# Transformer and delta-rule kernel on one core: the value product ahead of the transposes of k and q, with fill matmuls, a reciprocal root and a residual sum moved behind other work

## The reference

```
x = x + 0.5 * ffn(layernorm(x))
x = x + attn(layernorm(x))      # delta-rule memory, 64-wide keys
x = x + 0.5 * ffn(layernorm(x)) # the same weights as the first
```

```
h = shift_token(x);  q, k, v = split(h @ wqkv)        # 8 heads of 64
q = l2norm(q) * qs;  k = l2norm(k) * ksc;  q, k = rotary_xpos(q, k)
o = local_attention(q, k, v)                          # window of 128, own and previous block
x = x + o @ wo
h = layernorm(shift_token(x)) * lg + lb;  a, g = split(h @ w1 + b1)
x = x + (a * gelu(g)) @ w2 + b2
```

## Time and profile before

| | |
|---|---|
| median of 3 runs | 2738.12 us (2736.51 to 2740.71) |
| the profiled execution | 2735.22 us |
| its span on the core | 2733.4 us, granted TensorE clock 0.995 |
| PE matmuls busy | 2530.3 us (93%) |
| PE weight loads busy | 2233.3 us (82%) |
| DVE busy | 1997.0 us (73%) |
| ACT busy | 1857.7 us (68%) |
| POOL busy | 1514.3 us (55%) |

### The profile page before, as it was taken

The page is one execution under the profiler, slowest core; times in us unless marked ns, Lnnn a source line. Parts: engine busy times, 40 slices in busy tenths (PEclk is TensorE's granted clock), DMA queues, the critical chain, the costliest instruction groups (busy, mean ns, idle before and its releaser), DMA issues.

```text
span 2733.4 us, 79930 instructions
## 1 busy us (share of the span) xinstructions
PE 2530.3 (93%) x29664; PEld 2233.3 (82%) x29664; DVE 1997.0 (73%) x6533; ACT 1857.7 (68%) x5192; POOL 1514.3 (55%) x1767
## 2 busy tenths in 40 slices
PE   8899999998999999999999899999998999999999
PEld 7788888887888888888767788888887888888888
DVE  7777777776777777777656777777776777777776
ACT  6767777766676777666454777776666677766665
POOL 5565566655555565555213556665554566655555
PEclk9999999999999999999999999999999999999999
DMA  3122101003000000005100000000003100000000
GB/s 117 33 79 75 49 18 52 21 20 112 14 2 3 2 2 25 2 2 195 33 19 31 2 2 2 2 2 2 2 2 113 33 2 18 18 18 18 17 18 25
DMA packets 75954, 82.18 MB, mean 30 GB/s; under 512 B 37552, under 2 KB 61872, under 8 KB 74416
## 3 DMA queue, kind: packets, MB, share of 16 engines
q1 hardware_dynamic: 70176, 75.51, 8.5%
q10 hardware_dynamic: 5392, 1.56, 0.2%
HBM read 49.53 MB, written 26.74 MB: 28 GB/s over the span
## 4 chain that ended last, share of the span: by engine, by line
PE 43%; DVE 18%; POOL 17%; ACT 9%; issue 7%; DMA 4%; SPq 1%; DVEq 0%; POOLq 0%; ACTq 0%
POOL pr L631 7%; PE bank L1111 6%; PE bank L1113 6%; PE bank L1112 6%; POOL r L618 5%; DVE pr L1714 5%; PE bank L1222 5%; PE bank L1345 4%; PE bank L1147 4%; DMA stt<-stt 3%; ACT pr L815 3%; POOL t L621 3%; PE bank L1510 2%; PE bank L1174 2%; DVE t L1680 2%
## 5 line engine op out<-in xcount | busy, mean ns | idle before, releaser
L631 POOL TENSOR_TENSOR pr<-pr,rden 128x384 f32<-128x384 f32 (+1 forms) x512 | 433.2, 861 | 502.1 <-DVE rden L1723 501.3
L815 ACT ACTIVATE pr<-pr,nb 128x192 f32<-128x192 f32 (+1 forms) x1024 | 440.2, 431 | 119.3 <-DVE nb L1714 119.2
L1111 PE MATMUL bank<-h2T,w 128*128 128x256 f32 x1408 | 405.2, 288 | 8.1 <-DVE h2T L1750 1.2
L1112 PE MATMUL bank<-h2T,w 128*128 128x256 f32 x1408 | 394.7, 280 | 0.0
L1113 PE MATMUL bank<-h2T,w 128*128 128x256 f32 x1408 | 394.6, 280 | 0.0
L1714 DVE CUSTOM_DVE_ANT_0 pr<-bank,maskb,r 128x192 f32<-128x192 f32 (+1 forms) x1024 | 356.6, 395 | 19.7 <-issue 9.9
L663 POOL TENSOR_TENSOR uTl<-t,uTh 128x256 fp32r<-128x256 f32 x288 | 219.1, 761 | 208.5 <-ACT uTh L911 207.8
L1111 PE MATMUL bank<-wqkv,hT 128*128 128x512 f32 x768 | 309.9, 404 | 12.4 <-DMA wqkv<-wqkv_split 8.5
L1812 DVE SCALAR_TENSOR_TENSOR t<-bank,b,t 128x256 f32<-128x256 f32 (+1 forms) x384 | 183.2, 480 | 174.5 <-ACT t L896 103.3
L1112 PE MATMUL bank<-wqkv,hT 128*128 128x512 f32 x768 | 304.4, 396 | 0.0
L1113 PE MATMUL bank<-wqkv,hT 128*128 128x512 f32 x768 | 302.1, 393 | 0.0
(11 more groups left out here) (244 smaller groups left out, 7326.2 us busy)
## 6 DMA issues: line engine op xcount, KB each, us to landing
wqkv<-wqkv_split SPq DMA_DIRECT2D x18, 512.0 KB, 7.2
w<-w_split SPq DMA_DIRECT2D x3, 2816.0 KB, 9.9
Y<-in_x SPq DMA_DIRECT2D x8, 512.0 KB, 8.0
out<-Y SPq DMA_DIRECT2D x8, 512.0 KB, 3.9
stt<-stt SPq DMA_DIRECT2D x224, 3.0 KB
h<-out SPq DMA_DIRECT2D x7, 512.0 KB, 4.0
out<-h SPq DMA_DIRECT2D x7, 512.0 KB, 3.0
stt<-stt SPq DMA_DIRECT2D x192, 0.0 KB
```

What stands on the lines that cost most here:

```text
L631: e.tensor_tensor(probs(j, t), probs(j, t), rden[:, 2 * j:2 * j + 2].unsqueeze(2).to_broadcast([P, 2, w]), ALU.mult).then_inc(pn_done, 1)
L815: last = e.activation(probs(j, t)[:, g, :], probs(j, t)[:, g, :], ACT.Exp, bias=nb[:, hd:hd + 1], scale=-1.0, accum_out=den[:, hd:hd + 1])
L1111: e.matmul(out, left[0], right[0], start=first, stop=False)
L1112: e.matmul(out, left[0], right[1], start=False, stop=False)
```

## The change

The PE places the value product ahead of the transposes of k and q, takes all W2 units out of the place between the scores and the projections, and puts six of them (in the last tile nine, as before) behind the transposes. DVE does the residual sum of the W2 product one tile later, behind the fourth score instruction pair, puts A0 ahead of the attention residual, and does the second addition of the value product's halves behind the first scores. ACT copies the value product and h2T of the last tile ahead of kT and qT. POOL computes LayerNorm's power behind all four normalisings instead of behind the first.

```
 POOL
                     for j in range(4):
-                        if t == 3 and j == 1:
-                            LN(L, b, 0)
                         NP(L, b, t, j)
+                    if t == 3:
+                        LN(L, b, 0)
 ACT
                     if ahead2:
                         A0(*ahead2)
+                    if t == 3:
+                        O(L, b, t)
+                        H2T(L, b, 0)
                     if ahead:
                         A2(*ahead)
                     if L == 0 and b < B - 1 and 0 < t < 3:
                         for k in (2 * t - 2, 2 * t - 1):
                             entry_apply(b + 1, k)
-                    if t == 3:
-                        O(L, b, t)
-                        H2T(L, b, 0)
 PE
-                    cuts = ((5, 9, UNITS, UNITS), (0, 4, UNITS, UNITS), (0, 4, UNITS, UNITS), (0, 4, 8, UNITS))[t]
+                    cuts = ((5, 5, 11, UNITS), (0, 0, 11, UNITS), (0, 0, 11, UNITS), (0, 0, 8, UNITS))[t]
...
                     fill(1)
                     if ahead2:
                         A0(*ahead2)
-                    if ahead:
-                        A2(*ahead, 0)
-                        A2(*ahead, 1)
                     if t:
                         PV(L, b, t)
                     else:
                         PV_first(L, b, t)
+                    if ahead:
+                        A2(*ahead, 0)
+                        A2(*ahead, 1)
                     fill(2)
 DVE
                     if t > 1:
-                        O_add(L, b, t - 1)
+                        O_add(L, b, t - 1, 0)
                     S(L, b, t, 0)
+                    if t > 1:
+                        O_add(L, b, t - 1, 1)
                     if t:
                         O(L, b, t - 1)
                     S(L, b, t, 1)
...
                     S(L, b, t, 3)
+                    if prev and t:
+                        W2(*prev, t - 1)
                     for j in range(1, 4):
...
+                    if ahead2:
+                        A0(*ahead2)
                     if t:
                         WO(L, b, t - 1)
                         halves(L, b, t - 1)
-                    if prev and t < 3:
-                        W2(*prev, t)
-                    if ahead2:
-                        A0(*ahead2)
...
                     if t == 3:
                         LN_apply(L, b, 0)
-                        O_add(L, b, t)
+                        for i in pair:
+                            O_add(L, b, t, i)
                         O(L, b, t)
                         if prev:
                             W2(*prev, t)
```

More of the change, by code:

```diff
@@ L1723, in R, with O_add @@
                 e.reciprocal(rden[:, 2 * j:2 * j + 2], den[:, 2 * j:2 * j + 2]).then_inc(rden_done, 1)
[L1725 to L1730, removed]
+            def O_add(L, b, t, i):
+                cols = slice(2 * P * i, 2 * P * i + 2 * P)
+                e.wait_ge(o_first, at(o_first, sums(L, b, t) + i + 1))
+                e.tensor_tensor(o_sum[:, cols], bank[O_BANK[1]][:, cols], o_sum[:, cols], ALU.add).then_inc(o_added, 1)
             def O(L, b, t):
@@ L1958, in sequence @@
                         halves(L, b, t - 1)
[L1959 to L1962, removed]
                     if L == 0 and b == 0 and t < 3:
```

## The result

The changed kernel takes 2852.1 us (2850.51 to 2855.8) against 2738.01 us (2736.51 to 2740.71) for the kernel before: a ratio of 1.0417, 95% interval 1.0399 to 1.0436, slower by 114 us. The direction was forecast, the size was not: the forecast was 2812 us, and the range ended at 2850.

A forecast was written before the change was run, and what follows sets the result against it. A ring of dependences, not PE, bounds the kernel: 28 sequences at +2.0 us (56), odd sequences 4 and 1, first pass 13, together 74 on 2735.2, plus 2.9 to the median: 2812 us; range 2765 to 2850.

The forecast's parts named there:

- The ring: In the attention tiles PE, POOL, DVE and ACT wait for each other in a circle; any lengthened piece is paid in full.
- N: The end of POOL's last normalising in a tile; before the change the next S came 7.0 us later.
- Rival 1: The value product starts right behind PTE (N + 2.65) without waiting for DVE: faster, 2706 us; chance 0.10.
- S: The start of the first scores on DVE in a tile; from it to the third 1/sum took 4.7 us before.
- S at N + 7.7: DVE's first scores follow its first addition by 0.34 us, at N + 7.7 instead of N + 7.0: +0.7 us.
- The split of the two additions: Only the first addition stands ahead of S; the second (0.34 us) moves behind S in tiles 2 and 3.
- The feed-forward residual, +0.34 us in each tile: On DVE the residual moves from idle time into the stretch from S to N in tiles 1, 2 and 3.
- Tile 3, +0.4: N moves by 0.1 us against S, and the first W1 product comes at N + 9.9 instead of N + 9.6.
- rival 3: POOL's normalising locks out DVE's rotation addition in tiles 1 to 3, 0.6 us each: 2862 us; chance 0.05.
- The first pass, 13 us: ACT's normalisation of x delays its copy of the value product by 0.95 us, in two tiles of seven sequences.
- Rival 2: DVE's moved work (0.34 and 0.68 us) is absorbed because POOL or ACT is late anyway: 2783 us; chance 0.10.
- Rival 4: Tile 1's residual statistics, read in tile 3, arrive late; 0.6 us of DVE waiting per sequence gives 2829 us; chance 0.05.

The follow-up runs named there:

- the best version: Changed kernel with A0 behind attention residual, additions together, ACT's normalisation and LayerNorm's power earlier, feed-forward residual of tiles 1 and 2 in its own tile: 2666.22 us.

## Why the prediction was right or wrong

- *The ring bounds the kernel, not PE.* Right: PE's busy time hardly moved (2530.3 to 2547.3 us) while the span grew by 115 us.
- *The product waits for PTE, ACT's A0, DVE's A0 and the residual, and starts at N + 3.8.* Right: N + 3.81, and the other order on DVE took the loss away. Rival 1, that the product does not wait for DVE, was wrong for this change. Where its condition was brought about, with A0 behind, the kernel measured 2730 us against its 2706; S follows PE's scores there too (1909.28 to 1910.30), which the rival's sum does not have either.
- *"its next instruction 0.34 us behind that: S at N + 7.7".* This is the step that failed. S was at N + 8.26. The prediction let DVE's first scores follow the first addition after 0.34 us; they came 0.86 us behind it (1992.95 and 1993.81), because they wait for PE's scores. These start at 1992.78, right behind ACT's copy of qT (1992.05 + 0.59 = 1992.64), and reach DVE 1.03 us after their start. The prediction had a term for this stretch only in tile 0, "some 0.7 of their half's 0.94 us", and there it measured 1.02: from the end of the copy of qT to S it was 1.16 us (2041.68 to 2042.84), where 0.81 had been forecast. In the kernel before, the stretch was covered; PE's scores of tile 3 started there at 1911.15 (the line from PE's timeline is below), 0.31 us before ACT began the copy of the product (1911.46) and 0.72 before DVE's additions (1911.87), so that DVE's first scores at 1912.55 came when both additions were done. The change put the transposes last, so that scores and additions start together (1992.78 and 1992.95), and the cover was gone. It accounts for 0.3 us in tile 0 and 0.5 in each of tiles 1 and 2, about 1.3 of the 1.55 us missed per sequence. That PE's scores bind S is shown by the second addition, which was put ahead of S without moving it; that the old order covered the stretch is read from the timelines, and no run changed that stretch by itself.

```profile
1911.15 1.63 PE L1174 MATMUL bank<-kT,qT 64*64 64x192 f32 x48
```

- *"The split of the two additions is already in this".* Wrong in sign. It was to bring S 0.34 us forward; it brought nothing there, as the additions fit into DVE's wait, and behind S it cost 0.34 us and 0.24 more through ACT's oT. The second figure was not in the sum; in tile 2 it is the other 0.24 of the 1.55 us missed. Putting the additions together gave 32 us back.
- *The feed-forward residual, +0.34 us in each tile.* Right where the row shows it: from S to the third 1/sum it is 5.03 us in tile 1 against 4.68 (the 1/sum at 2047.87), and 5.61 in tile 2 (1983.27 - 1977.66) against 4.69, with the addition and oT.
- *Taking the four units away gains nothing.* Right as far as the rows show it: PE waits 0.28 and 0.20 us for DVE's first scores at the projections (1978.57 and 1980.40). Not seen was what the units mean for the rest: with thirteen of them ahead of the product and four more ahead of the projections PE comes to it too late, and the residual a tile later does not go together with units ahead of the projections (3129 us).
- *Tile 3, +0.4.* The sum is right at +0.37, its two parts are not, and that they cancel is luck. From S to N it grew by 0.32 us and not by 0.1 (N is 2000.26 + 2.04 = 2002.30, so 8.49 us behind S; before it was 1920.72 - 1912.55 = 8.17): ACT's second oT copy costs its 0.24 here too. From N to the first W1 product it took 9.67 us and not 9.9; the product started at 2006.11, again N + 3.81. The rotation's addition (L1687) took 0.69 us there, no longer 1.27 as in the earlier trace rows: POOL's second normalising ended at 1999.83 and the addition started at 2000.14; POOL's third, which started behind it at 2000.26, took 1.26 us instead of 0.83. The rule that of a DVE instruction with two SBUF inputs and a GpSimd instruction that reads SBUF the one that starts first keeps the other out (the Trainium skill, SBUF — State Buffer, "SBUF: two separate sides") went the way the forecast took it; the trace agrees, and rival 3 did not come.
- *The first pass, 13 us.* 8 were measured: half of each late copy falls into DVE's wait for PE's scores, the stretch that the prediction left out.
- *Rival 2, that the moved DVE work is absorbed,* fell: the residual shows with its full 0.34 us, and the second addition cost 32 us, more than its own duration (28 x 2 x 0.34 = 19).
- *Rival 4, late statistics,* shows no new wait: DVE waited 30.7 us for them in all, 39.1 in the kernel before.

The bounds were made from the terms of the sum and not from what was left out of it. The terms themselves reach from 2777 (2812 - 13 - 14 - 8) to 2833 (2812 + 13 + 8); nothing in the working stands for the 12 us from there to the stated 2845. The only allowance for another link (a hop of 0.1 us) was far smaller than the one that had been hidden.

## What to carry to other kernels

Before moving a product ahead of another in one queue, write down every wait of the moved product and where in the other engines' queues the releasing instruction stands: DVE's order cost nothing while the product stood behind the transposes, and 122 us once it stood ahead of them. When the last link of a ring is replaced, price the whole way of the next candidate from start to release, not only the link in front of the old one; a stretch that was covered (here 1.03 us from PE's scores to DVE) appears in full. Look for the gain stretch by stretch: the best version is faster than the kernel before in tile 0 and behind the last scores, and not in the tiles that were studied first. And a place in a queue is good or bad only with its neighbours: LayerNorm's power behind the normalisings gained 10 us in one version and lost 13 in another.

## What the runs showed that was not expected

- PE's scores reach DVE late: in the changed kernel DVE's first scores started 1.03 us after PE's (1992.78 to 1993.81), although the matmuls they read are three quarters of a half that takes about 0.8 us. The same stretch is 1.02 us in tile 1 of the next sequence (2041.82 to 2042.84), in the kernel where the product alone was moved (1928.70 to 1929.72) and in the one with A0 behind (1909.28 to 1910.30), and S comes at its end each time.
- An accumulating product whose parts wait for different copies can start ahead of the later one: in the kernel with A0 behind, it started 0.2 us before PTE ended and took its usual 1.57 us.
- In the kernel with the units back, with PE still for 3.6 us in each of 90 tiles, the granted clock of the execution was 0.922, against 0.997 in the kernel without that edit. Between 1890 and 1920 us it was 0.89, 0.77 and 0.91 of 2.4 GHz in three stretches of 10 us, so that the lower of the two levels, 1.2 GHz, was granted for part of each.
